# Query constants by memset, 0/1 matrices on VectorE and a looped general section in a cross-attention + expert kernel

## The reference, cut to what matters

```python
x = x + xattn(layernorm(x), ctx, ctx, mask)      # x 1024x128, ctx 6404x128
x = x + moe_ffn(layernorm(x))                    # 8 experts, top 2, 128 -> 512 -> 128, gelu
def xattn(query, key, value, mask, ...):         # 16 heads of 8
    q, k, v = heads(query @ Wq.T + bq), heads(key @ Wk.T + bk), heads(value @ Wv.T + bv)
    scores = where(mask, lowest, q @ k.T / sqrt(8))
    return (softmax(scores) @ v merged) @ Wo.T + bo
```

## Time and profile before

| what | value |
|---|---|
| median of 3 runs | 335.9 us (335.01 to 337.93) |
| profiled execution | 335.63 us, of which 333.9 us lie between its first and its last instruction (the span) |
| mean granted clock of TensorE | 0.916 |
| busy: PE, DVE, ACT, POOL | 260.5, 170.1, 230.8, 84.7 us |
| transfers | 29.57 MB, 89 GB/s over the span |

### The profile page before, as it was taken

One profiled execution on the slowest core, in us unless ns is written; L12 is line 12 of the kernel. 1 busy time (PEld: TensorE's weight loads), 2 busy tenths in 40 slices (PEclk: granted clock), 3 DMA queues, 4 the chain that ended last, 5 costly groups with the idle time before them and its releaser, 6 DMA issues.

```text
span 333.9 us, 6252 instructions
## 1 busy us (share of the span) xinstructions
PE 260.5 (78%) x1855; PEld 130.2 (39%) x1856; DVE 170.1 (51%) x420; ACT 230.8 (69%) x364; POOL 84.7 (25%) x138
## 2 busy tenths in 40 slices
PE   2587866499999999989899999986484169999940
PEld 2464535122222221212222222235473169999940
DVE  4638966044544535353545454438751047676622
ACT  4366564389999999999999999961794024555520
POOL 8899002100000000000000000402057504444430
PEclk9999895599999999999999999997789559999995
DMA  6999790001101010101001010199201170111115
GB/s 195 381 273 399 291 206 17 5 23 23 34 5 39 0 39 12 28 12 28 18 22 26 14 32 7 39 377 276 36 33 48 48 183 26 32 33 34 31 32 187
DMA packets 29091, 29.57 MB, mean 89 GB/s; under 512 B 15357, under 2 KB 22929, under 8 KB 28944
## 3 DMA queue, kind: packets, MB, share of 16 engines
q1 hardware_dynamic: 27456, 26.21, 26.1%
q0 software_dynamic: 1616, 3.13, 3.2%
HBM read 21.62 MB, written 7.45 MB: 87 GB/s over the span
## 4 chain that ended last, share of the span: by engine, by line
issue 27%; PE 26%; ACT 20%; DVE 7%; DMA 7%; another core or an unknown queue 4%; POOL 3%; SPq 2%; ACTq 1%; DVEq 1%; POOLq 1%
ACT w2T L995 9%; ACT arenaB L995 9%; PE bank L1278 6%; DMA mask_u<-in_mask_BxSxS_bk_dram 5%; PE bank L1397 5%; PE bank L1260 5%; PE bank L1405 3%; DVE arenaB L900 2%; PE bank L1345 2%; PE bank L1169 1%; DMA arenaA<-ys_dram 1%; DVE arenaB L906 1%; PE bank L1355 1%; DVEq L895 1%
## 5 line engine op out<-in xcount | busy, mean ns | idle before, releaser
L717 DVE TENSOR_TENSOR arenaA<-bank,arenaA 128x512 f32<-128x512 f32 x80 | 55.2, 690 | 76.4 <-PE bank L1278 76.4
L995 ACT ACTIVATE arenaB<-bank 128x1024 f32<-128x1024 f32 x80 | 77.5, 1021 | 8.3 <-PE bank L1260 6.2
L995 ACT ACTIVATE w2T<-bank 128x1024 f32<-128x1024 f32 x80 | 76.7, 1030 | 1.3
L1260 PE MATMUL bank<-qS,keys 64*128 64x512 bf16 x324 | 63.2, 389 | 10.1 <-ACT w2T L995 5.7
L1025 ACT ACTIVATE mask_u<-bank,arenaB 128x128 f32<-128x128 f32 x92 | 26.2, 368 | 39.7 <-PE bank L1397 39.7
L1260 PEld LDWEIGHTS bank<-qS,keys 64*128 64x128 bf16 x324 | 15.4, 93 | 97.1 <-ACT w2T L995 49.4
L1278 PE MATMUL bank<-arenaB,vcur 128*32 128x512 f32 x320 | 42.6, 605 | 1.0
L1278 PE MATMUL bank<-w2T,vcur 128*32 128x512 f32 x320 | 42.6, 605 | 0.0
L411 POOL CAST keep<-flags 128x1 f32 x11 | 2.1, 187 | 141.0 <-DVE arenaC L628 140.3
L478 POOL DMA_INDIRECT ys_dram<-arenaB,mask_u x23 | 22.2, 964 | 36.3 <-DVE arenaB L906 36.3
L1397 PE MATMUL bank<-arenaB 128*128 128x128 f32 x184 | 27.4, 296 | 2.8 <-DVE arenaB L892 2.5
(11 more groups left out here) (301 smaller groups left out, 325.7 us busy)
## 6 DMA issues: line engine op xcount, KB each, us to landing
mask_u<-in_L_ffn_w_dram SPq DMA_DIRECT2D x2, 2048.0 KB, 10.6
mask_u<-in_mask_BxSxS_bk_dram SPq DMA_DIRECT2D x6, 560.5 KB, 16.0
ctx_sb<-in_ctx_dram SPq DMA_DIRECT2D x3, 768.0 KB, 13.2
qS<-qparts_dram SPq DMA_DIRECT2D x4, 448.0 KB
mask_u<-in_mask_BxSxS_bk_dram SPq DMA_DIRECT2D x6, 240.0 KB, 11.6
keys_in<-kparts_dram SPq DMA_DIRECT2D x40, 32.0 KB
mask_u<-in_mask_BxSxS_bk_dram SPq DMA_DIRECT2D x1, 1121.0 KB, 8.4
xs_dram<-w1T SPq DMA_DIRECT2D x2, 520.0 KB, 16.8
```

What stands on the lines that cost most here:

```text
L717: nc.vector.tensor_tensor(a, bank[:, 4 + k % 2, :], a, ALU.add).then_inc(s["ac"], 1)
L995: nc.scalar.activation(probs[u % 8], bank[:, 2 * (u % 2):2 * (u % 2) + 2, :].rearrange("p a b -> p (a b)"), ACT.Exp, scale=SCALE).then_inc ...
L1260: last = mm(bank[:, 2 * (u % 2) + a, :], keys[rows, g, :], qS[rows, g, cols], start=not hides, stop=True, tile_position=(64 * a, 0))
```

## The change

Four edits go together.

- The constant rows of `qS` are written by two POOL memsets (8 x 4096 f32) instead of one memset and two transfers.
- `pick` (the comparison over 128 x 3072) moves from POOL to DVE, behind the first mask slice. The subtraction that gives query part 2 moves from POOL to DVE. `qres` moves ahead of mask slice 4, from behind it. POOL keeps the cast to part 1.
- The mask cast of the first tile moves from POOL to ACT, behind ACT's clearing of the accumulators (L977) and ahead of the square root of the bound (L979).
- The general section on PE has one unit pair written out, inside a loop over t, instead of 16 units; POOL copies a slice of `qS` for each turn. PE loads one value (`general`) ahead of the branch, and loads n and `partial` behind the first products, just ahead of `pe.If(partial)`.

```diff
@@ POOL
-            nc.gpsimd.memset(ones_rows, BF16_ONES).then_inc(s["ones_in"], 1)
-            pool.wait_ge(s["ones_in"], 1)
             for w in range(2):
-                pool.dma_start(qS[64 * w:64 * w + 8, :, :].bitcast(F32),
-                               ones_rows.rearrange("p (a q) -> p a q", a=1).broadcast_to([8, G, 512])).then_inc(s["qzero"], 16)
+                nc.gpsimd.memset(qS[64 * w:64 * w + 8, :, :].bitcast(F32), BF16_ONES).then_inc(s["qzero"], 1)
...
-            pool.wait_ge(s["rowkey"], len(COMBOS) + 4)
-            nc.gpsimd.tensor_scalar(pick, rowkey, iota_p[:, :], None, ALU.is_equal).then_inc(s["pick"], 1)
             pool.wait_ge(s["q_sb"], 2)
             nc.gpsimd.tensor_copy(qparts[:, 1, :], qres).then_inc(s["q_sb"], 1)
-            pool.wait_ge(s["q_sb"], 3)
-            nc.gpsimd.tensor_tensor(qparts[:, 2, :], qres, qparts[:, 1, :], ALU.subtract).then_inc(s["q_sb"], 1)
             pool.wait_ge(s["plan_ready"], 1)
             nc.gpsimd.memset(s2row[:, :], float(S2)).then_inc(s["s2"], 1)
-            first = pool.value_load(plan[0:1, 0:1], min_val=0, max_val=T - 1)
-            nc.gpsimd.tensor_copy(mbf[:, :, :], mask_u8[:, :, bass.ds(first * P, P)]).then_inc(s["mb"], 1)
@@ DVE
-            ors(0, 1, 5)
+            ors(0, 1, 2)
+            dve.wait_ge(s["rowkey"], len(COMBOS) + 4)
+            nc.vector.tensor_scalar(pick, rowkey, iota_p[:, :], None, ALU.is_equal).then_inc(s["pick"], 1)
+            ors(0, 2, 4)
             dve.wait_ge(s["qk_sb"], 1)
             dve.wait_ge(s["q_sb"], 1)
             nc.vector.scalar_tensor_tensor(qres, qp, qk_col[:, 0:1], qparts[:, 0, :], ALU.add, ALU.subtract).then_inc(s["q_sb"], 1)
-            ors(0, 5, QT)
+            ors(0, 4, 6)
+            dve.wait_ge(s["q_sb"], 3)
+            nc.vector.tensor_tensor(qparts[:, 2, :], qres, qparts[:, 1, :], ALU.subtract).then_inc(s["q_sb"], 1)
+            ors(0, 6, QT)
@@ ACT
             nc.scalar.activation(arenaA[:, :].rearrange("p (a b) -> p a b", b=512), ones[:, :].rearrange("p (a b) -> p a b", a=1).broadcast_to([P, 8, 512]), ACT.Copy, scale=0.0).then_inc(s["ac"], 1)
+            act.wait_ge(s["plan_ready"], 1)
+            first = act.value_load(plan[0:1, 0:1], min_val=0, max_val=T - 1)
+            nc.scalar.activation(mbf[:, :, :], mask_u8[:, :, bass.ds(first * P, P)], ACT.Copy).then_inc(s["mb"], 1)
             act.wait_ge(s["bd"], 7)
...
@@ PE
             pe.wait_ge(s["gen_ready"], 1)
-            n = pe.value_load(plan[0:1, 64:65], min_val=1, max_val=T)
             general = pe.value_load(plan[0:1, 65:66], min_val=0, max_val=1)
-            partial = pe.value_load(plan[0:1, 66:67], min_val=0, max_val=T)
             with pe.If(general):
+                n_max = pe.value_load(plan[0:1, 64:65], min_val=1, max_val=T)
...
-                    for u in range(16):
-                        t, hh = u // 2, u % 2
-                        pe.wait_ge(s["m_red"], i * 16 + u + 1)
-                        for a in range(2):
+                    with pe.Fori(0, QT) as t:
+                        pe.wait_ge(s["m_qc"], i * 8 + t + 1)
+                        for hh in range(2):
...
+            n = pe.value_load(plan[0:1, 64:65], min_val=1, max_val=T)
+            partial = pe.value_load(plan[0:1, 66:67], min_val=0, max_val=T)
             with pe.If(partial):
```

More of the change, by code:

```diff
@@ L222, in build @@
                  "gt gtexp gxr gmid rdy gT_ps gT_sb hps hact yps yacc b2ps outs vinit sp_at pool_at dve_at pe_at hs "
-                 "qn_ps kn_ps bd bd_ps bd_sqrt bd_row kones sqr cc_ps cc_sb kk_ps wk_sb xs_fill fill rows scat T_ps T_sb stg rank_ps slot tile_tab acc0 acc1 fin tconst s2 bias kzero vzero kb_ps kb_sb qk_rows qk_ps qk_sb ones_in qsqr rowkey pick k0_ps "
+                 "qn_ps kn_ps bd bd_ps bd_sqrt bd_row kones sqr cc_ps cc_sb kk_ps wk_sb xs_fill fill rows scat T_ps T_sb stg rank_ps slot tile_tab acc0 acc1 fin tconst s2 bias kzero vzero kb_ps kb_sb qk_rows qk_ps qk_sb m_qc qsqr rowkey pick k0_ps "
                  "kc m_kc").split()
@@ L427, in _ @@
                     mask_tile(i, tile_in(plan[0:1, bass.ds(i, 1)], s["m_cb"], s["m_kv"], i + 1))
+                    with pool.Fori(0, QT) as t:
+                        pool.wait_ge(s["m_qk"], i * 16 + t * 2 + 17)
+                        nc.gpsimd.tensor_copy(qcur, qS[:, :, bass.ds(t * P, P)]).then_inc(s["m_qc"], 1)
                 tile_in(plan[0:1, 0:1], s["m_cb"], s["m_kv"], n + 1)
@@ L980, in _ @@
             nc.scalar.preload_act_table(ACT.Exp)
-            act.wait_ge(s["plan_ready"], 1)
             n = act.value_load(plan[0:1, 64:65], min_val=1, max_val=T)
@@ L1209, in _ @@
                 pe.wait_ge(s["qr"], 64)
-                pe.wait_ge(s["qzero"], 32)
+                pe.wait_ge(s["qzero"], 2)
                 pe.sem_inc(s["m_kv"], 1)
@@ L1215, in _ @@
                 project(0, s["m_cb"], s["m_kv"], False)
-                with pe.Fori(0, n) as i:
+                with pe.Fori(0, n_max) as i:
                     pe.wait_ge(s["m_kc"], i + 2)
+                    pe.sem_inc(s["pe_at"], 1)
                     pe.wait_ge(s["m_mb"], i + 1)
-                    for u in range(16):
-                        t, hh = u // 2, u % 2
-                        pe.wait_ge(s["m_red"], i * 16 + u + 1)
-                        for a in range(2):
-                            o = bank[:, 2 * hh + a, :]
-                            mm(o, nbig[:, :], mbf[:, t, :].rearrange("p (a k) -> p a k", a=1).broadcast_to([P, 4, P]), start=True, stop=False)
-                            for b in range(4):
-                                pair, rows = 4 * hh + b, slice(64 * a, 64 * a + 64)
-                                last = mm(o[:, b * P:(b + 1) * P], qS[rows, pair, t * P:(t + 1) * P], keys[rows, pair, :], start=False, stop=(b == 3), tile_position=(64 * a, 0))
-                        last.then_inc(s["m_qk"], 1)
-                        if u == 3:
-                            pe.wait_ge(s["m_kch"], i * 4 + 4)
-                            project(i + 1, s["m_cb"], s["m_kv"], False)
+                    pe.sem_inc(s["pe_at"], 1)
+                    with pe.Fori(0, QT) as t:
+                        pe.wait_ge(s["m_qc"], i * 8 + t + 1)
+                        for hh in range(2):
+                            pe.wait_ge(s["m_red"], i * 16 + t * 2 + hh + 1)
+                            for a in range(2):
+                                o = bank[:, 2 * hh + a, :]
+                                mm(o, nbig[:, :], mbf[:, bass.ds(t, 1), :].broadcast_to([P, 4, P]), start=True, stop=False)
+                                for b in range(4):
+                                    pair, rows = 4 * hh + b, slice(64 * a, 64 * a + 64)
+                                    last = mm(o[:, b * P:(b + 1) * P], qcur[rows, pair, :], keys[rows, pair, :], start=False, stop=(b == 3), tile_position=(64 * a, 0))
+                            last.then_inc(s["m_qk"], 1)
+                    pe.wait_ge(s["m_kch"], i * 4 + 4)
+                    project(i + 1, s["m_cb"], s["m_kv"], False)
                 pe.wait_ge(s["m_fin"], 5)
```

9 lines of the change are left out of this document (4 added, 5 removed).

## The result

The changed kernel takes 333.29 us (median of 12 runs, 332.35 to 335.28) against 337.07 for the kernel before in the same comparison (12 runs, 335.01 to 339.68): a ratio of 0.9896, 95% interval 0.9865 to 0.9928. That is faster by 1.0%, by the ratio 3.5 us. The forecast was 328.6, with a range of 326.0 to 332.2, and a gain of 7.2; the direction was right, half the gain came, and the time lies outside the range. Of the 4.7 us between forecast and time, 1.2 are the starting point: the forecast stood on the 335.9 of three runs, and the kernel before has 337.07 over twelve. The profiled execution took 333.22 us with a span of 331.5.

The account below looks back on a forecast made before the run. The loop was taken as bound by ACT's exponentials, so only its start could move: 2.9 (branch, loads, clock) + 3.5 (front) + 0.8 (mask cast) = 7.2 us, giving 328.6 us, range 326.0 to 332.2.

Parts of the forecast that it names:

- The first branch: PE's jump over the general section: 0.1 to 0.4 us instead of 3675 ns, so hides start 3.86 us earlier.
- The stall: PE's wait for instructions at the general section's branch: gone, with the second branch, over the unused tile loop, staying at 418 ns.
- Rival 1: PE's second branch finds its target missing after the code moves: 3.3 us come back, 332.0 us; chance 0.1.
- The loads: Two PE value loads ahead of the second branch, with nothing hiding them: a cost of 1.4 us.
- The clock: TensorE rises to full clock during the hides, before the first exponential: 0.45 us gained of a possible 1.28.
- The transfers: Without two SBUF-to-SBUF copies, the stretch at 158 GB/s runs at 400 and the mask lands 2.57 us earlier.
- DVE and POOL: The chain up to the numbers of block 0: 3.5 us earlier, bounds -1.5 (a loss) and 4.3.
- rival 2: POOL's memsets hold `pick`, so DVE's chain gains nothing: 331.9 us; chance 0.14.
- From the numbers to the plan: PE's counts and chunk work ahead of the plan: the 3.5 us carried through whole to `plan_ready`.
- The mask cast: Moved off POOL, it frees DVE's first context copy, gaining 0.77 us; about 1.05 on ACT, hidden.

Follow-up runs that it names:

- e2: The changed kernel without PE's unused loop for partly masked tiles and the branch over it; 329.12 us, ratio 0.9784.
- e4: The changed kernel with 64 never-run products added behind the loop of PE's general section; 329.75 us.
- e5: e4 with PE's loads of n and partial put back ahead of the first branch; 328.92 us, ratio 0.9785.
- e8: The changed kernel with 32 never-run products added behind the loop of PE's general section; 329.71 us.
- e7: e5 with the constant rows filled by one memset and two SBUF-to-SBUF transfers, as before the change; 330.8 us.
- e6: e5 with POOL waiting for `pick` before its two long memsets; 326.92 us, ratio 0.9716.
- e3: The kernel before with the edits on POOL, DVE and ACT alone, PE's general section and loads unchanged; 333.75 us, ratio 0.9888.
- e9b: e5 with POOL's two long memsets behind its cast of the query rest instead of ahead; 325.6 us, ratio 0.9678.
- e10: The changed kernel with 8 never-run products added behind the loop of PE's general section; 331.02 us.

## Why the prediction was wrong, point by point

*The first branch:* right. It takes 226 ns where 100 to 400 were forecast, and is out of the way before the shift row; hides follow at once.

*The stall:* wrong, and this is the step that failed. The sum took the second branch over at its old 418 ns: "both kernels reach the target from a neighbouring stretch and the 418 ns row is for this very jump". It cost 3609. Rival 1, *the stall only moves*, had the mechanism and was given 0.1. The row of 418 ns was read as a price of the jump, while it is one of the place where the jump lies, and the change moved all the code behind the section some 283 instructions towards the front. The pads show it: the same jump costs 0.33, 0.42, 2.4, 3.5 or 3.6 us. Rival 1 put its price at 3.3 us. It is 3.3 at the third exponential, 5.0 at the end of the first turn with what the clock adds, and 4.2 by medians (e2). Without the stall the gain is 7.3 us (e2, by its ratio; 5.4 to 9.2) where 7.2 were forecast. That the two agree is partly luck, since the terms below were off.

*The loads:* forecast 1.4 us on the path. Putting them back ahead of the first branch shortened the gap ahead of the third exponential by 1.2 us (e4 to e5) and the first turn by 0.2 to 1.1.

*The clock:* it was forecast that without a hole it would rise during the hides. It did, at 57 us, and then fell again in the new hole. This part was open in both directions and the forecast gave it 0.45 us of gain; it turned into some 1.7 of loss. What half clock costs there shows in e4 and e8, where both branches are short: in e4 the clock fell from 61 to 64, in e8 it stayed up, and the first turn ends at 76.5 and 75.6. Here is the same stretch of e4, then of e8:

```profile
62.00:63.00 1.00, 1.00 (x6) 0.20 (x8) 0.90 (x4) 1.00 (x2) 0.00 (x0) 0.50 0.00 0
62.00:63.00 1.00, 1.00 (x10) 0.11 (x6) 0.91 (x3) 1.00 (x2) 0.00 (x0) 1.00 0.03 8
```

That is 0.9 us for some 3 us at half clock; the changed kernel had twice as much, and the 1.7 fit.

*The transfers:* right. 397 GB/s where 158 were; 2.1 us at the numbers (e7), against 2.57 forecast for the landing.

*DVE and POOL:* 2.9 us at the numbers instead of 3.5. Two sizes were off and half cancelled. `pick` was taken at one element a cycle, 3.35 us, from an instruction of 128 columns; it runs at two, 1.8 us (e6). And it was held up by the first memset, which the row of 375 ns had announced; the prediction had counted that hold in its bounds at 1 to 2 us, and the hold of both memsets as rival 2. And DVE waited 0.9 us for POOL's cast, which the forecast had finished in time: it stood behind the memsets, of which the second took 1.5 us longer, and itself took 2.2 us beside DVE's ORs against 1.04 with DVE idle (e6).

```profile
15.25 5.14 DVE L550 TENSOR_SCALAR w1T<-arenaB,iota_p 128x3072 bf16<-128x3072 f32 x1 [0.68 <-POOL shift_rows L378]
15.27 8.57 POOL L380 MEMSET qS<- 8x4096 f32 x2
```

The Trainium skill (SBUF — State Buffer, section Who interferes with whom) says that the one which comes second is blocked for the whole instruction. The block is borne out on both sides, `pick` for 3.3 us and the second memset for 1.5. The order is not: `pick` shows 0.02 us ahead of the first memset and waited for it all the same, so that starts as close as these don't tell who will wait.

*From the numbers to the plan:* the 2.9 us became 2.1. PE's count of the second mask block waited longer for DVE (2.86 us of idle time against 1.37 before), and what came behind it ran at half clock. After, and as the last line the same two matmuls before:

```profile
41.52 0.53 PE L1081 MATMUL bank<-onesb,w2T 128*128 128x1 bf16 x15 [2.86 <-DVE w2T L535]
...
43.55 1.65 PE L1148 MATMUL bank<-ctx_sb,wk_turned 128*128 128x384 f32 x2
...
44.00:45.00 1.00, 1.00 (x3) 0.21 (x3) 0.23 (x2) 0.02 (x1) 0.00 (x0) 0.50 0.91 182
...
46.41 0.91 PE L1147 MATMUL bank<-ctx_sb,wk_turned 128*128 128x384 f32 x2
```

They took 0.91 us before, at full clock, and 1.65 now. The prediction carried the 3.5 us through with "it is not the chunks that bind"; the clock was left out there.

*The mask cast:* right, 1.06 to 0.23 us on DVE, and the cast on ACT (1.04 us at 49.2) hid behind its wait for the bound, 1.4 us of which were left.

Together: 2.1 + 0.8 at the shift row (57.44 to 54.49). By the times of e3 about that much reached the end, but the profiles show only 0.5 (e3) and 0.9 us (changed kernel) at the first turn; how the rest of the 3.5 us comes about stays open. What the PE edit gained at the hides, 4.4 of the 7.4 us at the first exponential, was given back by the second branch, the loads and the clock.

## What to carry to other kernels

A taken branch over a long stretch of unrun code cost PE 0.2 to 0.4 us here, or 3.4 to 3.7, once 2.4, by where the code lies, and any edit ahead of it can turn the one into the other; so look at the sequencer's branches before and after, and pad or shorten the code until all of them are short. Sixty-four products that never run were worth 3.5 us here (333.29 to 329.75, the latter one run). The hole on TensorE cost twice, the second time, it seems, in half clock behind it. And when work moves from POOL to DVE, look at what POOL does at the same time: a long memset and a tensor_scalar of DVE took turns here, and the order in which POOL did its work (e6, e9b) decided what that cost.

## What the runs showed of the hardware that was not expected

- A branch can take a time between short and long: 2447 ns (e10), between 326 (e8) and 3609 (changed kernel). By the block model the target's block was already on its way.
- Two transfers of 128 KB from eight rows into eight rows held the traffic of all queues at 117 to 177 GB/s for 4 us (22 to 26 us of e7), with the DMA engines shown as fully busy; about 400 GB/s without them (e5).
- A memset of POOL writes 8 x 4096 f32 in 3.50 us; eight rows take it as long as 128 would at the rate of the earlier trace rows.
- The part behind the tile loop, the same code in all kernels, took 110.5 to 112.3 us.
